# The second gate chunk of layer 0: from a VectorE maximum to two ScalarE copies and a GpSimd addition

## The reference

```python
def _lrelu(v):
    return jnp.where(v >= 0, v, NEG_SLOPE * v)        # NEG_SLOPE = 0.2
e = jnp.concatenate([x[row], x[col]], axis=-1)        # 128 values an edge
g1 = _lrelu(jnp.einsum('ef,hgf->heg', e, gate_w1))    # 4 heads x 64
alpha = _lrelu(jnp.einsum('heg,hog->heo', g1, gate_w2))
a = w_edge * jnp.exp(alpha)
m1 = _lrelu(jnp.einsum('ef,hgf->heg', e, msg_w1))     # 4 heads x 128
beta = _lrelu(jnp.einsum('heg,hog->heo', m1, msg_w2))
out_h = segment_sum(alpha_n * beta)                   # alpha_n: a over its sum per row
```

## Time and profile before

| | |
|---|---|
| median of 3 runs | 6655.64 us (6654.76 to 6658.46) |
| the profiled execution | 6656.1 us, its span 6654.2 us |
| mean granted clock of TensorE over the span | 0.791 of 2.4 GHz |
| layer 0's blocks | about 668 to 4215 us of the span |
| DVE / PE / POOL / ACT busy over the span | 72% / 66% / 57% / 40% |

### The profile page before, as it was taken

How to read it: one execution, slowest core, us unless ns; L and a number is a source line. 1 busy time by engine, 2 the same in 40 slices (tenths; PEclk the granted TensorE clock), 3 DMA queues, 4 the chain that set the end, 5 groups by cost and what they waited for, 6 DMA issues and landing times.

```text
span 6654.2 us, 117791 instructions
## 1 busy us (share of the span) xinstructions
PE 4382.8 (66%) x24069; PEld 2598.3 (39%) x24069; DVE 4799.1 (72%) x10127; ACT 2634.2 (40%) x6054; POOL 3779.0 (57%) x3799
## 2 busy tenths in 40 slices
PE   3611999999999999999999999233333333333334
PEld 1211444444444444444444444133333333333333
DVE  6986788888888888888888888755555555555554
ACT  1200666666666666666666666200000000000000
POOL 0100555555555555555555555177777777777774
PEclk9955999999999999999999999655555555555555
DMA  8301333333333333333333333222222222222222
GB/s 237 152 0 33 73 72 72 72 72 72 72 72 72 72 72 72 72 72 72 71 71 72 72 71 72 70 51 50 51 50 51 51 50 51 50 51 51 50 51 59
DMA packets 485530, 452.11 MB, mean 68 GB/s; under 512 B 281672, under 2 KB 372041, under 8 KB 483593
## 3 DMA queue, kind: packets, MB, share of 16 engines
q0 software_dynamic: 137360, 180.87, 16.9%
q1 hardware_dynamic: 321118, 246.02, 13.3%
q10 hardware_dynamic: 27008, 24.74, 1.5%
HBM read 363.66 MB, written 87.55 MB: 68 GB/s over the span
## 4 chain that ended last, share of the span: by engine, by line
PE 27%; DVE 26%; issue 20%; POOL 19%; DMA 3%; ACT 3%; POOLq 1%; DVEq 1%; SPq 0%; ACTq 0%
POOL ends L749 11%; POOL work L749 8%; PE ps_beta L1620 6%; DVE work L1158 6%; PE ps_beta L1628 5%; PE ps_hidden L1568 5%; DVE work L1287 5%; PE ps_hidden L1569 4%; DVE beta L1163 4%; DVE ends_hot L1147 3%; PE ps_sum L1639 3%; DVE terms L1179 2%; ACT scaled L813 2%; DVE parts L1179 2%; PE ps_T L1557 1%
## 5 line engine op out<-in xcount | busy, mean ns | idle before, releaser
L1767 PE MATMUL ps_beta<-work,equal 128*128 128x128 f32 x3232 | 834.1, 440 | 1548.5 <-DVE work L1492 1548.5
L652 POOL DMA_INDIRECT ends<-split_table,src_sb x808 | 775.7, 960 | 1456.0 <-issue 1429.7
L1767 PEld LDWEIGHTS ps_beta<-work,equal 128*128 128x128 f32 x3232 | 719.4, 328 | 1663.4 <-issue 1523.3
L1158 DVE TENSOR_TENSOR work<-work,ps_hidden 128x512 f32<-128x512 f32 x1616 | 1099.7, 680 | 256.6 <-ACT work L813 256.0
L1568 PE MATMUL ps_hidden<-ends_parts,w_high 128*128 128x512 f32 x2424 | 1109.4, 458 | 1.2 <-ACT ends_hot L860 1.2
L813 ACT ACTIVATE work<-ps_hidden 128x512 f32<-128x512 f32 x1616 | 965.0, 597 | 325.1 <-DVE work L1158 316.0
L652 POOL DMA_INDIRECT ends<-split_table,gather_sb x808 | 805.5, 997 | 502.4 <-issue 374.6
L749 POOL DMA_INDIRECT work<-src_table,src_sb x808 | 814.8, 1008 | 336.6 <-issue 239.2
L749 POOL DMA_INDIRECT ends<-src_table,gather_sb x808 | 863.5, 1069 | 245.6 <-issue 245.3
L1620 PE MATMUL ps_beta<-work,msg_w_sb 128*64 128x512 f32 x3232 | 871.6, 617 | 192.8 <-DVE work L1158 192.8
L1569 PE MATMUL ps_hidden<-ends_hot,window 128*128 128x512 f32 x2424 | 958.9, 396 | 0.0
(11 more groups left out here) (156 smaller groups left out, 6189.6 us busy)
## 6 DMA issues: line engine op xcount, KB each, us to landing
window<-window_table SPq DMA_DIRECT2D x808, 96.2 KB
dst_rows_sb<-by_src SPq DMA_DIRECT2D x404, 128.0 KB
window_table<-parts SPq DMA_DIRECT2D x50, 770.0 KB, 3.3
ends<-in_edge_attr SPq DMA_DIRECT2D x202, 128.0 KB
key_rows<-in_edge_attr SPq DMA_DIRECT2D x202, 128.0 KB
sums<-key_rows POOLq DMA_DIRECT2D x404, 32.6 KB
sums<-parts ACTq DMA_DIRECT2D x10, 1305.0 KB, 14.9
ends<-split_table,src_sb POOLq DMA_INDIRECT x808
```

Source lines behind the costliest of these rows:

```text
L652: pool.indirect_dma_start(out=ends[m][:, t, :], out_offset=None, in_=split_table, in_offset=bass.IndirectOffsetOnAxis(ap=src_windows[m][:, ...
L1158: nc.vector.tensor_tensor(hidden[k][:, :], scaled[k % NL][:, :], ps_hidden[k % NL][:, :], ALU.max).then_inc(hidden_ready, 1)
L1767: last = nc.tensor.matmul(ps_beta[0][0:WIN, 0:W1], hot[m % 2][:, t, :].bitcast(F32), terms1_windows[m][:, t, :], start=(m == 0 and t == 0) ...
```

## The change

Chunk 1, the second gate chunk, gets another rectifier than the other five. ScalarE writes two copies of the bank, `sloped` = 0.2 v and `raised` = relu(0.8 v) (`raise_chunk`), and GpSimd adds them into `hidden[1]` (`rectify_second`); 0.2 v + relu(0.8 v) is v for v above zero and 0.2 v below. VectorE no longer touches chunk 1. Two semaphores are new: `raised_ready`, raised by both copies, on which GpSimd and TensorE's chunk 4 (which uses the same bank, `drained`) wait; and `added_ready`, raised by the addition, on which the gate product waits, and ScalarE before it overwrites the two copies in the next block. VectorE's count `hidden_ready` has five steps a block instead of six, which `rectified` recomputes. The two copies have 512 elements each of a spare part of `parts[1]`.

```diff
+        raised, sloped = spare_flat[:, 0:B], spare_flat[:, B:2 * B]
...
+        def drained(eng, b, k):
+
+            if k == 4:
+                wait(eng, raised_ready, 2 * b + 2)
+            elif k >= NL:
+                wait(eng, hidden_ready, rectified(b, k - NL))
+            else:
+                wait(eng, hidden_ready, rectified(b - 1, k + NL))
...
+            def rectify_second(b):
+
+                pool.wait_ge(raised_ready, 2 * b + 2)
+                wait(pool, gates_done, b)
+                nc.gpsimd.tensor_tensor(hidden[1][:, :], raised, sloped, ALU.add).then_inc(added_ready, 1)
+
             def edges0_windows(b, quad, m):
                 more = not (isinstance(b, int) and b >= NB - 3)
...
                 if more:
                     gather0_tiles((m + 3) % 4, T // 2)
+                rectify_second(b)
                 if adds:
                     add_rows(quad - 1, 2 * m - 3)
...
+            def raise_chunk(b):
+
+                act.wait_ge(hidden_done, NK * b + 2)
+                wait(act, added_ready, b)
+                nc.scalar.activation(sloped, ps_hidden[1][:, :], ACT.Copy, scale=SLOPE).then_inc(raised_ready, 1)
+                nc.scalar.activation(raised, ps_hidden[1][:, :], ACT.Relu, scale=1.0 - SLOPE).then_inc(raised_ready, 1)
...
                 scale_alpha(b)
                 if not is_last(b):
-                    scale_chunk(b + 1, 1)
+                    raise_chunk(b + 1)
                 exp_alpha(b)
...
                                         ALU.max).then_inc(alpha_ready, 1)
-                if not is_last(b):
-                    rectify_chunk_windows(b + 1, 1)
...
             def gate_product(b):
 
-                pe.wait_ge(hidden_ready, NK * b + 2)
+                pe.wait_ge(hidden_ready, rectified(b, 0))
+                pe.wait_ge(added_ready, b + 1)
                 wait(pe, gates_copied, b)
```

More of the change, by code:

```diff
@@ L178, in gnn @@
         gates_T = parts_flat[1][:, ZW + NB * T + T * W0:ZW + NB * T + T * W0 + 2 * P]
+        spare_flat = parts_flat[1][:, ZW + NB * T + T * W0 + 2 * P:ZW + NB * T + T * W0 + 2 * P + 2 * B]
+        raised, sloped = spare_flat[:, 0:B], spare_flat[:, B:2 * B]
         hot_quad = [equal[0][:, :, :].rearrange("p t e -> p (t e)")[:, m * T * WIN0:(m + 1) * T * WIN0]
@@ L317, in gnn @@
         gates_copied = sem("gates_copied")
+        raised_ready = sem("raised_ready")
+        added_ready = sem("added_ready")
         gates_turned = sem("gates_turned")
@@ L352, in early, with rectified @@
             return isinstance(b, int) and b < 2
+        NV = NK - 1
+        def rectified(b, k):
+            return NV * b + (0 if k == 0 else k - 1) + 1
+        def drained(eng, b, k):
[5 more added lines that the diff above has]
+                wait(eng, hidden_ready, rectified(b - 1, k + NL))
         def first_four(b):
@@ L860, in copy_ends, with scale_chunk_windows @@
                 nc.scalar.activation(ends_hot[j][0:D, :], ps_T[0:D, :], ACT.Copy).then_inc(ends_hot_ready, 1)
+            def scale_chunk_windows(b, k):
+                act.wait_ge(hidden_done, NK * b + k + 1)
+                if k == 4:
+                    wait(act, hidden_ready, rectified(b - 1, 4))
+                elif k >= NL:
+                    wait(act, hidden_ready, rectified(b, k - NL))
+                else:
+                    wait(act, hidden_ready, rectified(b - 1, k + NL))
+                nc.scalar.activation(scaled[k % NL][:, :], ps_hidden[k % NL][:, :], ACT.Copy,
+                                     scale=SLOPE).then_inc(scaled_ready, 1)
+            def raise_chunk(b):
[3 more added lines that the diff above has]
+                nc.scalar.activation(raised, ps_hidden[1][:, :], ACT.Relu, scale=1.0 - SLOPE).then_inc(raised_ready, 1)
             def scale_pair(b, a):
@@ L895, in edges0_windows @@
                     scale_pair(b - 1, 1)
-                scale_chunk(b, 2)
+                scale_chunk_windows(b, 2)
                 if m == 1 and not first_four(b):
                     copy_quad(quad - 1)
-                scale_chunk(b, 3)
+                scale_chunk_windows(b, 3)
                 if not is_last(b):
                     copy_ends(b + 1, 1 - j)
-                scale_chunk(b, 4)
+                scale_chunk_windows(b, 4)
                 copy_gates(b)
                 scale_pair(b, 0)
-                scale_chunk(b, 5)
+                scale_chunk_windows(b, 5)
                 if not is_last(b):
-                    scale_chunk(b + 1, 0)
+                    scale_chunk_windows(b + 1, 0)
                 scale_alpha(b)
                 if not is_last(b):
-                    scale_chunk(b + 1, 1)
+                    raise_chunk(b + 1)
                 exp_alpha(b)
@@ L953, in _ @@
                 copy_ends(0, 0)
-                scale_chunk(0, 0)
-                scale_chunk(0, 1)
+                scale_chunk_windows(0, 0)
+                raise_chunk(0)
                 fours(act, edges0_windows)
@@ L1151, in rectify_chunk_windows @@
             def rectify_chunk_windows(b, k):
-                dve.wait_ge(scaled_ready, NK * b + k + 1)
+                dve.wait_ge(scaled_ready, rectified(b, k))
                 if not (isinstance(b, int) and b == 0):
-                    if k < 2:
+                    if k == 0:
                         dve.wait_ge(gates_done, b)
@@ L1380, in _ @@
                 rectify_chunk_windows(0, 0)
-                rectify_chunk_windows(0, 1)
                 fours(dve, edges0_windows)
@@ L1565, in first_product_windows @@
                     pe.wait_ge(window_in[j], 48 * (half + 1))
-                wait(pe, hidden_ready, NK * b + k + 1 - NL)
+                drained(pe, b, k)
                 o = ps_hidden[k % NL][:, :]
@@ L1615, in pair_product @@
             def pair_product(b, a):
-                pe.wait_ge(hidden_ready, NK * b + 2 * a + 4)
+                pe.wait_ge(hidden_ready, rectified(b, 2 * a + 3))
                 wait(pe, terms_ready, 2 * (b - 1) + a + 1)
```

## The result

The changed kernel takes 10,013.6 us (median of 4 runs, 10,013.3 to 10,015.3), the kernel before 6,655.9. The ratio is 1.504 (95% interval 1.502 to 1.507). The forecast of 10,190 us is 1.8% above that.

The account below looks back on a forecast made before the run. TensorE, 93% busy, was fullest in layer 0; after the change a serial chain through GpSimd's gathers sets each block: 15.34 + 2.2 = 17.54 us; 404 x (17.54 - 8.765) - 16 = 3529 us more, 10,190 us, range 9,250 to 11,250 (own 9,700 to 10,850).

Parts of the forecast that it names:

- The bound and the gain: Layer 0: TensorE is fullest at 93%; removing VectorE's chunk 1 operation gains 0 us, at the most 246.
- The ring: Layer 0: gate product, pair products, chunk 2, weights, four gathers, addition, next gate product follow without overlap; 17.54 us a block.
- 1 weights to first gather: GpSimd in layer 0: time from the end of VectorE's weights to the first gather's start, 0.8 us a block.
- 2 four gathers: GpSimd in layer 0: first gather's start to last gather's end, now ahead of the addition, mean 5.29 us a block.
- 3 addition: GpSimd's 128x512 two-input addition of chunk 1's copies: 1.13 us at the copy's rate, ends 0.73 and 2.26.
- 5 and 6, at the full clock: Layer 0: gate product to weights of the same block, 7.54 us, plus the sum of four blocks, 0.48 a block.
- the lower clock: TensorE in layer 0: falls to 1.2 GHz before each gate product, 5 us of work at that clock; adds 2.2 us.
- Both clock rivals: TensorE's clock in layer 0 either stays full (9,296 us) or never comes back (11,207 us); chance 0.12 each.
- The first: TensorE's clock stays full in layer 0: a block of 15.34 us, time 9,296 us; chance 0.12.
- The second: TensorE's clock never comes back in layer 0: gate product to weights 11.8 us, block 20.07, time 11,207 us; chance 0.12.
- The addition not held by the gathers: GpSimd in layer 0: gathers issued early enough, addition ready before the gate product; 0 to 246 us faster; chance 0.04.
- the addition is dear beside VectorE or the transfers: GpSimd's addition takes 4 us instead of 1.13 beside VectorE or transfers; 1159 us more, 11,350 us; chance 0.04.

Follow-up runs that it names:

- the move of one line: Against the changed kernel, GpSimd's addition of chunk 1 stands ahead of the four gathers of its body instead of behind them: 6,866 us, ratio 1.0315 to the kernel before.
- the addition at the end of the body: Against the changed kernel, GpSimd adds block b+1's chunk 1 at the end of body b, behind the gathers, ahead of the last row transfer: 6,712 us, ratio 1.0082.

## Why the prediction was right, and where it was off

**The bound and the gain.** That VectorE's chunk 1 lay in a hole and its removal gives nothing: confirmed; with all of it gone the kernel took 6,690 us.

**The ring.** Confirmed by the timeline and by the move of one line. Piece by piece, in the numbering of the prediction:

| piece | predicted | measured |
|---|---|---|
| 1 weights to first gather | 0.8 | 0.78 and 0.83 |
| 2 four gathers | 5.75, 5.88, 4.84, 4.69 (mean 5.29) | 5.77, 5.88, 4.85, 4.71 (mean of all 5.32) |
| 3 addition | 1.13 | 1.29 |
| 4 hand-over | 0.1 | 0.1 |
| 5 and 6, at the full clock | 7.54 + 0.48 = 8.02 | 7.93 (50 matmuls in the pause) |
| the lower clock | 2.2 | 1.62 |
| a block | 17.54 | 17.07 |

**The addition** was the one cost that no row of before showed. Its width taken in proportion to a one-input copy was 0.16 us too little, 65 us in all. The Trainium skill's twice VectorE (GPSIMD Engine Reference, Performance versus the Vector engine) gave an estimate of 1.38; the trace has 1.29 against 0.69, 1.9 times, and agrees with it better than my estimate. The 1.68 of some rows is the same addition with the end of a row transfer in its row. My expectation for the addition at the end of the body put it down to VectorE, wrongly.

**The clock** was the term that I mis-sized, by 0.58 us a block or 234 us. I let the lower level last 5 us into the work; the rows of after have the rise 4.15 us behind the gate product. The one case of before already said so, and I misread it: 0.57 in the microsecond from 673 is 0.86 us at the lower level, so the rise came at 673.86, 4.0 us after the start and not 3.6. Work of 4.15 us at half speed loses 2.1; the measured 1.62 leaves about 0.45 that was caught by waits, where I had 0.3. No run measures that by itself. The fall came later here than at the end of layer 0 before: 4.9 us after the last matmul, there 2.6. It didn't matter, since the pause was longer still. Both clock rivals are excluded as the case at hand. The first is confirmed as a number, within 43 us: with the clock kept up the kernel took 9,339 us, where that rival had 9,296. The second's step of 11.8 us isn't derivable as it stands: 7.54 with 5.5 doubled is 13.0, and what should catch the rest isn't said.

The errors partly cancel, and that is luck: in a block -0.58 for the clock, -0.09 for steps 5 and 6, +0.16 for the addition and +0.03 for the gathers make -0.48, and the block was 17.07 us instead of 17.54. That is 190 us less. 26 us came on top outside layer 0, which the prediction had at nothing and for which no run gives a cause: 10,190 - 190 + 26 = 10,026, 12 from the measured time. The range of 9,700 to 10,850 named first isn't the plain sum of its three terms either (that is 9,500 to 11,290); the time lies in both.

**The signs.** TensorE was 58% busy, the clock 0.80, the first gather 0.8 us behind the weights and the addition straight behind the fourth gather, as announced. The gate product's idle time was longer than the 5 to 7 us: 2,869.5 / 404 = 7.1 on average. And its row names no releaser ("issue"); that it waits for the addition follows from its start 0.1 us behind the addition's end, from the semaphore, and from the rows with matmuls in the pause, which name L691.

**The other rivals.** The addition not held by the gathers was not what the change does, but as an experiment it gave 6,712 to 6,866 us and no gain, because the gain of VectorE's operation is nil. That the addition is dear beside VectorE or the transfers didn't show: from the end of what stood ahead of it, it took 1.3 us in every run with the whole addition.

## What to carry to other kernels

Before a piece of work is moved to an idle engine, ask what stands ahead of it in that engine's queue and what that is waiting for. GpSimd was idle for 45% of the stage, but its queue held four gathers which were released by a late stage of the block before, and that stage came behind that block's own gate product, which had waited for an addition too; 1.3 us of work cost 8.3. And an operation that lies in a hole of the busiest engine is worth nothing when it is taken away: look at the idle time before the next operation of that engine, not at its busy share.

## What the runs showed of the hardware

- A VectorE operation of 0.17 us which reads and writes SBUF took 0.76 when it started beside a GpSimd addition; in 197 such meetings of one run it ended 0.04 us behind the addition in the median. The addition kept its 1.3 us. VectorE's operations that read one input from PSUM ran beside additions at their usual 0.69 in the same trace, nearly 700 of them.
- GpSimd's row for an addition straight behind a row transfer began 0.29 to 0.38 us before the transfer's row ended (198 cases), and was longer by as much. Behind a gather the two rows met within 0.03 us.
- An addition of 128x512 took 1.29 us on GpSimd and 0.69 on VectorE; of 128x128 0.48 on GpSimd.
- TensorE's clock fell once in every block of a loop with a pause of 7.2 us on average and a block of 17.07, and still in one with a pause of 4.1 us and a block of 14.5. With 50 idle matmuls in the pause, which left 0.5 to 2.4 us of it, it fell in 2 of 404 blocks, and that was worth 675 us of 10,014 (648 of them in layer 0's blocks). With 36, which left 2.1 to 3.4 us in nearly all blocks, it fell in nearly two of three.
- How much a longer or shorter pause costs isn't just its length: with the clock's part, 1.43 us more ahead of the gate product made the block 1.69 longer, and 3.04 less made it 2.57 shorter.
